# All three earlier taps of a causal convolution on TensorE; shorter rings, and one product per chunk from POOL to VectorE

## The chip, the cores and the metric

One core of one Trainium2 chip runs the whole kernel in one launch, in float32. The metric is device time in microseconds, median of the runs. Engines are named as in the profile: PE is TensorE, PEld its weight loads, DVE VectorE, ACT ScalarE, POOL GpSimd, SP SyncE.

## The reference, cut to what matters

```python
h = layernorm(x) * (1 + ca) + sa                     # x: (2, 2048, 512)
h, gate = split(h @ in_proj_w.T)                     # E = 1024 channels each
h_c = conv(h, conv_w, taps=4, causal, per channel) + conv_b
h = silu(h_c)
dt, B, C = split(h @ x_proj_w.T)                     # 128, N = 16, 16
dt = softplus(dt @ dt_proj_w.T + dt_proj_b)
s[t] = s[t-1] * exp(dt[t] * A) + dt[t] * h[t] * B[t] # E x N states
y = sum_n(s[t] * C[t]) + h * D
x = x + ga * ((y * silu(gate)) @ out_proj_w.T)
x = x + gb * (layernorm(x) * (1 + cb) + sb) @ sum_r(factors[r]) / sqrt(8)   # + bias
```

The convolution has four taps per channel: `h_c[t] = w3 h[t] + w2 h[t-1] + w1 h[t-2] + w0 h[t-3] + b`.

## The kernel before, in words

The 2 x 2048 rows are cut into 16 chunks of 256 rows, in order of time, eight for each batch. A chunk is worked in 64 units: a unit is one of the 16 state indices n of one of four pairs of channel blocks (2 x 128 channels). Two units are a step s (32 steps a chunk), four are a quad g (16 quads a chunk). While the units of chunk c run, the same program carries the input side of chunk c+1 (projection, convolution, silu, dt, B and C) and the output side of chunk c-1 (gate, output projection, residual, second norm, the last matrix product). What stands at which step is written out by hand in tables and conditions on s and g; each engine runs its own list strictly in that order and waits on semaphores.

A unit goes like this. POOL makes `ub` = u * B for a whole quad at once (`make_ub`, two quads ahead, ring of three). ScalarE makes the decays exp(dt * A) in one of three PSUM banks (`decays`). VectorE runs the scan over 256 rows (`scan`, line 1426). The state is multiplied by C either on VectorE (`multiply_c`, line 1441, into `sc_d`, ring of three) or, for the last k units of a quad, on POOL (line 596, into `state_p`, ring of `P_RING` slots). The tables `EVEN_POOL`, `ODD_POOL` and so on give k for each quad; chunk 0 has FIRST_POOL, chunk 1 FOLD_POOL, chunk 15 LAST_POOL, and chunks 2 to 14 take EVEN and ODD in turn (2 is even). TensorE turns every product with a transposing matmul and adds it up in `y_bank` (`turn_states`, line 1010), and ScalarE copies the sum of a pair to `y_rows` (line 811).

The convolution of pair q of chunk c+1 passes four engines. TensorE projects h into PSUM (`project_h`, line 1085). ScalarE copies it to `pre` with the last three rows of the chunk before, and scales the PSUM bank by w3 and adds the bias (`copy_h`, line 775; it sets `pre_made`). VectorE adds the tap w0 (`taps`, line 1481, two instructions of 256 columns; `tap_done`). TensorE adds w1 and w2: for each of two channel blocks a matmul of 256 columns for each tap, with a diagonal matrix of the weights as the stationary side (`add_tap`, line 1068). ScalarE takes the tanh (line 787), VectorE finishes the silu into `hc` (`silu_before`, line 1490). For pairs 0 to 3 in the chunks after the first, `copy_h` and `taps` stand at steps 5, 7, 11, 13, `add_tap` at 6, 8, 12, 14, tanh and silu at 8, 10, 14, 16. The next `project_h` into a bank waits for that silu.

On the output side of chunk c-1, TensorE turns the summed y (`turn_sums`, line 1141, steps 4 to 7), VectorE gates it (`gate_sums`, line 1522), TensorE projects it out (`project_out`, line 1157, steps 9 to 15), and VectorE adds the residual (`residual_mixer`, line 1529, steps 15 and 17).

POOL also makes u = dt * h for each pair (`make_u`, line 545), three of them in groups 0, 2 and 3 of a chunk and one in group 13 for the next.

Of the kernel before, what the change touches and what calls it, by code (L numbers as in the profile page):

```python
# [22 lines left out]
ALU = mybir.AluOpType  # L23
# [4 lines left out]
E, N, TAPS, RANK_DT = 1024, 16, 4, 128  # L28
RANK = 8
EPS = 1e-5  # L30
ROWS = 256
# [4 lines left out]
PAIRS = KE // 2  # L36
# [3 lines left out]
QUAD = 4  # L40
QUADS = UNITS // QUAD
UB_RING = 3
D_RING = 3
DVE_TAPS = 1
PE_TAPS = range(DVE_TAPS, TAPS - 1)
TAP_STEPS = 2 * DVE_TAPS
H_RING = 3
# [5 lines left out]
SILU_AT = ({7: 0, 9: 1, 12: 2, 14: 3}, {8: 0, 10: 1, 14: 2, 16: 3})  # L53
P_RING = 8
U_PAIRS = 3
H_TILES, Z_TILES = 3, 3
DT_PAIRS = 5
EVEN_POOL = (2, 2, 2, 2, 2, 2, 2, 2, 2, 2, 2, 1, 1, 1, 1, 1)
ODD_POOL = (2, 2, 2, 2, 1, 2, 2, 2, 2, 2, 2, 1, 1, 1, 1, 1)
FIRST_POOL = (2, 2, 1, 1, 1, 1, 1, 2, 1, 1, 1, 1, 1, 1, 1, 1)  # L60
# [104 lines left out]
def build(nc, x, win_m, xp_t, dt_t, wo_t, chan, cond_t, wmod, factors, bias, out):  # L165
# [11 lines left out]
    with ExitStack() as ctx:  # L177
# [6 lines left out]
        def sem(name):  # L184
            return ctx.enter_context(nc.semaphore(name))
# [82 lines left out]
        xa_loaded, bn_a, stats_a, norm_a, z_a = sem("xa_loaded"), sem("bn_a"), sem("stats_a"), sem("norm_a"), sem("z_a")  # L268
        pre_made, tap_done, tapped, diag_made, tanh_h_made, skip_made = sem("pre_made"), sem("tap_done"), sem("tapped"), sem("diag_made"), sem("tanh_h_made"), sem("skip_made")
        pair_read = sem("pair_read")  # L270
# [29 lines left out]
        def h_lane(c, q):  # L300

            return bank_c[q % 2] if c == 0 and q >= 2 else bank_a[q % 2]
# [210 lines left out]
        def _(pool):  # L513
# [27 lines left out]
            def make_u(c, q):  # L541

                pair, k = PAIRS * c + q, slice(2 * q, 2 * q + 2)
                pool.wait_ge(dt_made, pair + 1)
                pool.tensor_tensor(u[:, pair % U_PAIRS, :, :], dt[:, pair % DT_PAIRS, :, :], hc[:, k, :], ALU.mult).then_inc(u_made, 1)

# [103 lines left out]
            def one_round(c, par, la, lc):  # L650
                for g in range(QUADS):
# [9 lines left out]
                    multiply_c(quad)  # L661
                    if g in (0, 2, 3):
                        make_u(c, max(g, 1))
                    if c == 0 and g in (4, 6, 8, 10, 12, 14):
# [328 lines left out]
        def _(pe):  # L993
# [67 lines left out]
            def add_tap(c, q):  # L1061

                if c == 0 and q == 0:
                    pe.wait_ge(diag_made, len(PE_TAPS))
                pe.wait_ge(tap_done, TAP_STEPS * (PAIRS * c + q + 1))
                for j in range(2):
# [341 lines left out]
        def _(dve):  # L1408
# [61 lines left out]

            def taps(c, q):

                bk = h_lane(c, q)
                dve.wait_ge(pre_made, PAIRS * c + q + 1)
                for k in range(DVE_TAPS):
                    for j in range(2):
                        e, part = 2 * q + j, bk[:, j * ROWS:(j + 1) * ROWS]
                        if k:

                            dve.wait_ge(tap_done, TAP_STEPS * (PAIRS * c + q) + 2 * (k - 1) + j + 1)  # L1480
                        dve.scalar_tensor_tensor(out=part, in0=pre[q % 2][:, j, k:k + ROWS], scalar=conv[:, e, k:k + 1],  # L1481
                                                 in1=part, op0=ALU.mult, op1=ALU.add).then_inc(tap_done, 1)

            def silu_before(c, q):
# [118 lines left out]
            last.then_inc(seam_zeroed, 1)  # L1603
            taps(0, 0)
            for q in range(1, PAIRS):
                taps(0, q)
                silu_before(0, q - 1)
# [7 lines left out]
            def one_round(c, par, la, lc):  # L1615
                for s in range(STEPS):
# [52 lines left out]
                    if la is not None:  # L1669
                        if a in SILU_AT[c > 0]:  # L1670
                            silu_before(c + 1, SILU_AT[c > 0][a])
                        if a in TAP_AT[c > 0]:
                            taps(c + 1, TAP_AT[c > 0][a])
                    if la is not None and s == 31:
# [55 lines left out]
```

## Time and profile before

| | |
|---|---|
| median of 3 runs | 2022.62 us (2021.11 to 2022.76) |
| the profiled execution, its time | 2025.55 us |
| its span, first to last instruction | 2023.8 us |
| mean granted TensorE clock | 0.973 |
| instructions | 29343 |

The span is what the trace covers; the time of an execution has about 1.8 us around it. A row of a timeline gives start, duration, engine, line and tiles; brackets give how long the engine stood idle before it and what released it. One matmul of the program stands as two records in the trace, so that a row with x8 is four matmuls. PEclk is the granted clock: 1.00 is 2.4 GHz and 0.50 is 1.2 GHz, and a window that mixes them has a value between. Busy time of a full engine can be less than its work, since starts overlap the end of the instruction before.

### The profile page before, as it was taken

To read this page: it belongs to the slowest core of one execution; us is meant where nothing else is said; L and a number is where in the kernel's file an instruction comes from. 1 tells how busy PE (TensorE), PEld (TensorE's weight loads), DVE (VectorE), ACT (ScalarE), POOL (GpSimd) and SP (SyncE) were. 2 spreads that over 40 slices of the span, in tenths; PEclk is the share of its full clock that TensorE was granted. 3 is DMA by queue.
4 is the path that set the end of the run, shared out by engine and by line. 5 is a ranking of instruction groups with operands and counts; after the bars stand their busy time and mean duration, and the time that the engine had idled before them with its cause. 6 is when DMAs were issued, how large, how long until landed. Compare 5 with 4: busy or idle time off the path is not lost.

```text
span 2023.8 us, 29343 instructions
## 1 busy us (share of the span) xinstructions
PE 1759.7 (87%) x9128; PEld 1312.2 (65%) x9128; DVE 1867.4 (92%) x2240; ACT 1517.1 (75%) x4646; POOL 1835.7 (91%) x925
## 2 busy tenths in 40 slices
PE   7985889889889898988989888898988899898798
PEld 5664757667576765757666675766757576676564
DVE  2799989999999999999999999999999999999995
ACT  3767778697877869777786977878787786878662
POOL 1789999999999999999998999999999999999992
PEclk9897999999999999999999999999999999999798
DMA  4656514132140412304042240403223040311200
GB/s 171 235 114 153 140 48 147 31 121 79 43 143 15 152 47 97 103 30 154 17 141 68 111 141 22 157 22 131 68 73 121 28 156 22 121 53 55 92 27 32
DMA packets 72001, 186.17 MB, mean 92 GB/s; under 512 B 6818, under 2 KB 8482, under 8 KB 63908
## 3 DMA queue, kind: packets, MB, share of 16 engines
q1 hardware_dynamic: 68148, 176.95, 26.3%
q0 software_dynamic: 3696, 7.34, 2.2%
q8 instruction: 73, 1.20, 0.2%
q14 instruction: 84, 0.69, 0.1%
HBM read 172.20 MB, written 12.06 MB: 91 GB/s over the span
## 4 chain that ended last, share of the span: by engine, by line
PE 42%; ACT 19%; POOL 15%; DVE 13%; issue 9%; DMA 1%; DVEq 0%; POOLq 0%; SPq 0%; ACTq 0%
PE y_bank L1010 10%; PE bank_a L1085 10%; PE bank_c L1157 9%; POOL ub L568 8%; ACT decay L722 7%; DVE decay L1426 5%; POOL state_p L596 5%; PE bank_c L1057 4%; DVE state_p L1426 3%; PE bank_a L1068 2%; ACT dt L835 2%; DVE sc_d L1441 2%; ACT L722 2%; ACT hT L737 2%; ACT L835 2%
## 5 line engine op out<-in xcount | busy, mean ns | idle before, releaser
L568 POOL TENSOR_TENSOR ub<-u,b_all 128x2048 f32<-128x2048 f32 x255 | 1160.4, 4551 | 48.5 <-DMA b_all<-bc_scratch 47.4
L722 ACT ACTIVATE decay<-dt,decay_rate 128x256 f32<-128x256 f32 (+1 forms) x2048 | 889.6, 466 | 36.0 <-DVE state_p L1426 34.3
L1426 DVE TENSOR_TENSOR_SCAN decay<-decay,carry,ub 128x512 f32<-128x512 f32 x610 | 763.7, 1277 | 25.8 <-ACT decay L722 23.8
L596 POOL TENSOR_TENSOR state_p<-state_p,c_all 128x1024 f32<-128x1024 f32 (+1 forms) x256 | 498.7, 1948 | 85.3 <-ACT carry L706 82.4
L1426 DVE TENSOR_TENSOR_SCAN state_p<-decay,carry,ub 128x512 f32<-128x512 f32 x414 | 527.4, 1274 | 9.3 <-ACT decay L722 7.2
L1010 PE MATMUL y_bank<-ident,sc_d 128*128 128x128 f32 x2440 | 362.5, 283 | 79.9 <-DVE sc_d L1441 79.5
L1441 DVE TENSOR_TENSOR sc_d<-decay,c_all 128x512 f32<-128x512 f32 x610 | 406.7, 671 | 0.0
L1010 PEld LDWEIGHTS y_bank<-ident,sc_d 128*128 128x128 f32 x2440 | 292.9, 145 | 146.1 <-DVE sc_d L1441 120.8
L706 ACT ACTIVATE carry<-decay 128x2 f32<-128x2 f32 x610 | 100.8, 165 | 264.8 <-DVE sc_d L1441 262.9
L1010 PEld LDWEIGHTS y_bank<-ident,state_p 128*128 128x128 f32 x1656 | 195.7, 143 | 126.9 <-POOL state_p L596 71.7
L1010 PE MATMUL y_bank<-ident,state_p 128*128 128x128 f32 x1656 | 231.0, 279 | 53.2 <-POOL state_p L596 52.0
L1085 PE MATMUL bank_a<-hT,win_h 128*128 128x256 f32 x992 | 240.5, 387 | 32.4 <-DVE hc L1490 30.0
L1057 PE MATMUL bank_c<-hT,win_z 128*128 128x256 f32 x960 | 230.7, 387 | 0.0
L1157 PE MATMUL bank_c<-wo,yg 128*128 128x512 f32 x480 | 223.8, 594 | 0.0
L1085 PEld LDWEIGHTS bank_a<-hT,win_h 128*128 128x128 f32 x992 | 182.3, 193 | 58.7 <-DVE hc L1490 35.7
L1057 PEld LDWEIGHTS bank_c<-hT,win_z 128*128 128x128 f32 x960 | 181.7, 196 | 22.6
L1068 PE MATMUL bank_a<-pre_z,tap_diag 128*128 128x256 f32 x496 | 120.4, 386 | 12.2 <-DVE bank_a L1481 12.2
L1157 PEld LDWEIGHTS bank_c<-wo,yg 128*128 128x128 f32 x480 | 86.6, 191 | 67.0 <-issue 64.8
L1068 PEld LDWEIGHTS bank_a<-pre_z,tap_diag 128*128 128x128 f32 x496 | 92.7, 191 | 39.8 <-DVE bank_a L1481 15.8
L1187 PE MATMUL bank_c<-ffn,hT 128*128 128x512 f32 x240 | 115.9, 605 | 0.0
L1001 PE MATMUL y_bank<-ident,skipped 128*128 128x128 f32 x256 | 42.9, 294 | 71.5 <-ACT y_rows L811 71.5
L718 ACT ACTIVATE decay<-ident 128x1 f32<-128x1 f32 x608 | 103.4, 170 | 0.1
(139 smaller groups left out, 1842.1 us busy)
## 6 DMA issues: line engine op xcount, KB each, us to landing
win_h<-win_m SPq DMA_DIRECT2D x128, 256.0 KB, 2.6
win_z<-win_m SPq DMA_DIRECT2D x128, 256.0 KB, 2.8
b_all<-bc_scratch SPq DMA_DIRECT2D x31, 1024.0 KB, 4.7
c_all<-bc_scratch SPq DMA_DIRECT2D x31, 1024.0 KB, 6.6
xa<-x SPq DMA_DIRECT2D x16, 512.0 KB, 5.0
xc<-x SPq DMA_DIRECT2D x16, 512.0 KB, 3.8
out<-xc SPq DMA_DIRECT2D x15, 512.0 KB, 4.0
ffn<-factors POOLq DMA_DIRECT2D x7, 1024.0 KB, 10.0
```

The source lines that it names most:

```text
L568: pool.tensor_tensor(ub[:, slot, :, :, :], u[:, (PAIRS * c + q) % U_PAIRS, :, :].unsqueeze(1).to_broadcast([P, QUAD, 2, ROWS]), b_all[:, n ...
L596: pool.tensor_tensor(part, part, c_all[:, n + QUAD - k:n + QUAD, :].unsqueeze(2).to_broadcast([P, k, 2, ROWS]), ALU.mult).then_inc(pooled, 1)
L718: act.activation(bk[:, ROWS:ROWS + 1], ident[:, 0:1], ACT.Copy, scale=0.0)
L722: last = act.activation(bk[:, j * ROWS + j:(j + 1) * ROWS], dt[:, pair % DT_PAIRS, j, j:], ACT.Exp, scale=decay_rate[:, e, n:n + 1])
L1010: last = pe.matmul(y_bank[:, at:at + P], tile[:, j, t * P:(t + 1) * P], ident[:, :], start=False, stop=last_of_pair, is_transpose=True, sk ...
L1057: last = pe.matmul(dst[:, j * ROWS:(j + 1) * ROWS], tile[:, k, :], hTc[:, k, :], start=(k == 0), stop=(k == KD - 1))
L1068: last = pe.matmul(h_lane(c, q)[:, j * ROWS:(j + 1) * ROWS], tap_diag[:, i, 2 * q + j, :], pre[q % 2][:, j, k:k + ROWS], start=False, stop ...
L1085: last = pe.matmul(h_lane(c, q)[:, j * ROWS:(j + 1) * ROWS], win_h[i % H_TILES][:, k, :], hT[c % H_RING][:, k, :], start=(k == 0 and j == ...
L1157: last = pe.matmul(bank_c[t][:, :], yg[:, k, t * P:(t + 1) * P], wo[:, k, :], start=(k == 0), stop=(k == KE - 1))
L1187: last = pe.matmul(bank_c[t][:, :], hT[c % H_RING][:, k, t * P:(t + 1) * P], ffn[:, k, :], start=False, stop=(k == KD - 1))
L1426: dve.tensor_tensor_scan(dst, bk[:, :], ub[:, quad % UB_RING, i, :, :].rearrange("p j r -> p (j r)"), carried_in[:, n, 2 * q:2 * q + 1], A ...
L1441: dve.tensor_tensor(sc_d[:, i % D_RING, :, :], bk[:, :].rearrange("p (j r) -> p j r", j=2), c_all[:, n:n + 1, :].to_broadcast([P, 2, ROWS] ...
```

## The change

The last VectorE tap goes to TensorE: `PE_TAPS` is now all of 0, 1, 2, and `add_tap` waits for `pre_made` instead of `tap_done`. `taps` and its semaphore are gone. `tap_diag`, the store of the diagonals, grows by one tap (4 KB a partition), and two rings shrink by 2 KB each: `P_RING` from 8 slots to 7, u from three pairs to two. With two pairs, `make_u` has a wait of its own on the sums made from the pair it overwrites, and the u of pair 3 is made in group 6 instead of 3. The tables for chunks 2 to 14 change: an even chunk has one product at quad 3 (was two), an odd one has one at quads 3 and 7 and two at quad 4 (was two, two and one); each such chunk has one product less on POOL and one more on VectorE.

```diff
-DVE_TAPS = 1
-PE_TAPS = range(DVE_TAPS, TAPS - 1)
-TAP_STEPS = 2 * DVE_TAPS
+PE_TAPS = range(TAPS - 1)
...
-P_RING = 8
-U_PAIRS = 3
+P_RING = 7
+U_PAIRS = 2
...
-EVEN_POOL = (2, 2, 2, 2, 2, 2, 2, 2, 2, 2, 2, 1, 1, 1, 1, 1)
+EVEN_POOL = (2, 2, 2, 1, 2, 2, 2, 2, 2, 2, 2, 1, 1, 1, 1, 1)
...
                 pool.wait_ge(dt_made, pair + 1)
+                if pair >= U_PAIRS:
+
+                    pool.wait_ge(ub_made, N // QUAD * (pair - U_PAIRS + 1) - 1)
...
-                    if g in (0, 2, 3):
-                        make_u(c, max(g, 1))
+                    if g in (0, 2, 6):
+                        make_u(c, {0: 1, 2: 2, 6: 3}[g])
...
-                pe.wait_ge(tap_done, TAP_STEPS * (PAIRS * c + q + 1))
+                pe.wait_ge(pre_made, PAIRS * c + q + 1)
...
-            def taps(c, q):
-
-                bk = h_lane(c, q)
-                dve.wait_ge(pre_made, PAIRS * c + q + 1)
-                for k in range(DVE_TAPS):
-                    for j in range(2):
-                        e, part = 2 * q + j, bk[:, j * ROWS:(j + 1) * ROWS]
...
-                        if a in TAP_AT[c > 0]:
-                            taps(c + 1, TAP_AT[c > 0][a])
```

On TensorE, from the first tap group of an even chunk (step 6) to the end of step 9, before the change; `y_rows` is the turned sum of chunk c-1, `sc_d` and `state_p` the products from VectorE and POOL:

```order
L1068 MATMUL bank_a<-pre_z,tap_diag 128x256 x4
L1010 MATMUL y_bank<-ident,sc_d 128x128 x4
L1141 MATMUL bank_c<-ident,y_rows 128x128 x4
L1010 MATMUL y_bank<-ident,state_p 128x128 x8
L1010 MATMUL y_bank<-ident,sc_d 128x128 x4
L1141 MATMUL bank_c<-ident,y_rows 128x128 x4
L1068 MATMUL bank_a<-pre_z,tap_diag 128x256 x4
L1085 MATMUL bank_a<-hT,win_h 128x256 x4
L1010 MATMUL y_bank<-ident,state_p 128x128 x8
L1001 MATMUL y_bank<-ident,skipped 128x128 x4
L1010 MATMUL y_bank<-ident,sc_d 128x128 x8
```

and of the change:

```order
L1069 MATMUL bank_a<-pre_z,tap_diag 128x256 x6
L1011 MATMUL y_bank<-ident,sc_d 128x128 x4
L1142 MATMUL bank_c<-ident,y_rows 128x128 x4
L1011 MATMUL y_bank<-ident,state_p 128x128 x8
L1011 MATMUL y_bank<-ident,sc_d 128x128 x8
L1142 MATMUL bank_c<-ident,y_rows 128x128 x4
L1069 MATMUL bank_a<-pre_z,tap_diag 128x256 x6
L1086 MATMUL bank_a<-hT,win_h 128x256 x4
L1011 MATMUL y_bank<-ident,state_p 128x128 x4
L1002 MATMUL y_bank<-ident,skipped 128x128 x4
L1011 MATMUL y_bank<-ident,sc_d 128x128 x8
```

Each tap group has six matmuls for four, and the four transposes of unit 14's product stand at step 7, among those of VectorE's products, instead of at step 9 among POOL's.

On VectorE, at step 7 and 8 of the same chunk, before the change; `yg<-bank_c` is the gating, `hc` the silu:

```order
L1426 SCALAR_TENSOR_TENSOR state_p<-decay,carry,ub 128x512
L1441 TENSOR_TENSOR sc_d<-decay,c_all 128x512
L1426 SCALAR_TENSOR_TENSOR state_p<-decay,carry,ub 128x512
L1522 TENSOR_TENSOR yg<-bank_c,yg 128x512
L1481 SCALAR_TENSOR_TENSOR bank_a<-pre_z,conv,bank_a 128x256 x2
L1426 SCALAR_TENSOR_TENSOR decay<-decay,carry,ub 128x512 x2
L1441 TENSOR_TENSOR sc_d<-decay,c_all 128x512
L1522 TENSOR_TENSOR yg<-bank_c,yg 128x512
L1490 SCALAR_TENSOR_TENSOR hc<-tanh_s,bank_a 128x512
```

and of the change:

```order
L1427 SCALAR_TENSOR_TENSOR decay<-decay,carry,ub 128x512
L1442 TENSOR_TENSOR sc_d<-decay,c_all 128x512
L1427 SCALAR_TENSOR_TENSOR state_p<-decay,carry,ub 128x512
L1442 TENSOR_TENSOR sc_d<-decay,c_all 128x512
L1510 TENSOR_TENSOR yg<-bank_c,yg 128x512
L1427 SCALAR_TENSOR_TENSOR decay<-decay,carry,ub 128x512 x2
L1442 TENSOR_TENSOR sc_d<-decay,c_all 128x512
L1510 TENSOR_TENSOR yg<-bank_c,yg 128x512
L1478 SCALAR_TENSOR_TENSOR hc<-tanh_s,bank_a 128x512
```

The two tap instructions are gone, and a second product stands ahead of the gating, since unit 14 is now scanned in a decay bank and multiplied by VectorE.

## Rows read from the trace of the kernel before

**Rows 1.** The page: span and busy time of each engine.

```profile
span 2023.8 us, 29343 instructions
...
PE 1759.7 (87%) x9128; PEld 1312.2 (65%) x9128; DVE 1867.4 (92%) x2240; ACT 1517.1 (75%) x4646; POOL 1835.7 (91%) x925
```

**Rows 2.** Groups by line and shape: count, busy us, mean ns, idle before.

```profile
L1441 DVE TENSOR_TENSOR sc_d<-decay,c_all 128x512 f32<-128x512 f32 x610 | 406.7, 671 | 0.0
L596 POOL TENSOR_TENSOR state_p<-state_p,c_all 128x1024 f32<-128x1024 f32 x158 | 372.8, 2359 | 66.4 <-ACT carry L706 63.5 <-DVE decay L1426 2.7
...
L596 POOL TENSOR_TENSOR state_p<-state_p,c_all 128x512 f32<-128x512 f32 x98 | 126.0, 1285 | 18.9 <-ACT carry L706 18.9
...
L545 POOL TENSOR_TENSOR u<-dt,hc 128x512 f32<-128x512 f32 x63 | 80.3, 1275 | 0.0
...
L1481 DVE SCALAR_TENSOR_TENSOR bank_a<-pre_z,conv,bank_a 128x256 f32<-128x256 f32 x124 | 54.0, 481 | 21.3 <-ACT bank_a L775 21.3
```

**Rows 3.** VectorE timelines, 747 to 992: start us, us, instructions.

```profile
751.37 0.69 DVE L1529 TENSOR_TENSOR xc<-bank_c,xc 128x512 f32<-128x512 f32 x1 [0.95 <-PE bank_c L1157]
...
827.75 0.69 DVE L1522 TENSOR_TENSOR yg<-bank_c,yg 128x512 f32<-128x512 f32 x1 [0.39 <-PE bank_c L1141]
...
831.90 0.87 DVE L1481 SCALAR_TENSOR_TENSOR bank_a<-pre_z,conv,bank_a 128x256 f32<-128x256 f32 x2
...
854.35 0.88 DVE L1481 SCALAR_TENSOR_TENSOR bank_a<-pre_z,conv,bank_a 128x256 f32<-128x256 f32 x2 [0.75 <-ACT bank_a L775]
...
869.78 0.69 DVE L1529 TENSOR_TENSOR xc<-bank_c,xc 128x512 f32<-128x512 f32 x1 [0.95 <-PE bank_c L1157]
...
989.88 0.69 DVE L1529 TENSOR_TENSOR xc<-bank_c,xc 128x512 f32<-128x512 f32 x1 [0.95 <-PE bank_c L1157]
```

**Rows 4.** TensorE timelines, 832 to 925 and 1041 to 1070.

```profile
836.97 1.99 PE L1085 MATMUL bank_a<-hT,win_h 128*128 128x256 f32 x8 [2.15 <-DVE hc L1490]
838.80 1.04 PE L1010 MATMUL y_bank<-ident,state_p 128*128 128x128 f32 x8
840.62 0.63 PE L1001 MATMUL y_bank<-ident,skipped 128*128 128x128 f32 x4 [0.78 <-ACT y_rows L811]
...
854.04 1.89 PE L1068 MATMUL bank_a<-pre_z,tap_diag 128*128 128x256 f32 x8
...
869.58 1.03 PE L1102 MATMUL bank_a<-hc,xp 128*128 128x256 f32 x4
...
1048.23 0.98 PE L1001 MATMUL y_bank<-ident,skipped 128*128 128x128 f32 x4 [2.04 <-ACT y_rows L811]
```

**Rows 5.** Chain that ended last, 800 to 925: start us, us, what.

```profile
831.99 0.79 DVE bank_a L1481 x2
...
870.61 0.89 PE y_bank L1010 x8
```

**Rows 6.** Windows near the starts of chunks 5, 6, 7 and 15.

```profile
core 0: us, PE busy (x) PEld busy (x) DVE busy (x) ACT busy (x) POOL busy (x), PEclk, DMA share, GB/s
...
689.00:695.00 6.00, 5.33 (x25) 4.90 (x26) 5.92 (x7) 3.85 (x14) 5.03 (x5) 0.72 0.64 226
809.00:815.00 6.00, 5.25 (x33) 4.82 (x34) 5.92 (x7) 4.96 (x19) 5.05 (x5) 1.00 0.80 271
927.00:933.00 6.00, 4.83 (x21) 4.26 (x22) 5.92 (x8) 3.96 (x14) 5.03 (x5) 0.72 0.74 255
...
1884.00:1890.00 6.00, 5.85 (x28) 5.30 (x29) 6.00 (x8) 3.86 (x15) 4.94 (x4) 0.72 0.59 208
```

**Rows 7.** Chain that ended last in the opening.

```profile
32.55 1.73 PE bank_a L1068 x8
...
45.70 2.00 PE bank_c L1068 x8
```

**Rows 8.** POOL timeline, 800 to 925.

```profile
873.36 2.36 POOL L596 TENSOR_TENSOR state_p<-state_p,c_all 128x1024 f32<-128x1024 f32 x1 [1.81 <-ACT carry L706]
```

**Rows 9.** A window over the ends of chunks 0 and 1, columns as in rows 6.

```profile
135.00:305.00 170.00, 128.64 (x669) 97.03 (x668) 157.07 (x176) 119.92 (x376) 168.38 (x82) 0.92 0.42 109
```

More of the change, by code:

```diff
@@ L53 @@
 SILU_AT = ({7: 0, 9: 1, 12: 2, 14: 3}, {8: 0, 10: 1, 14: 2, 16: 3})
-P_RING = 8
-U_PAIRS = 3
+P_RING = 7
+U_PAIRS = 2
 H_TILES, Z_TILES = 3, 3
 DT_PAIRS = 5
-EVEN_POOL = (2, 2, 2, 2, 2, 2, 2, 2, 2, 2, 2, 1, 1, 1, 1, 1)
-ODD_POOL = (2, 2, 2, 2, 1, 2, 2, 2, 2, 2, 2, 1, 1, 1, 1, 1)
+EVEN_POOL = (2, 2, 2, 1, 2, 2, 2, 2, 2, 2, 2, 1, 1, 1, 1, 1)
+ODD_POOL = (2, 2, 2, 1, 2, 2, 2, 1, 2, 2, 2, 1, 1, 1, 1, 1)
 FIRST_POOL = (2, 2, 1, 1, 1, 1, 1, 2, 1, 1, 1, 1, 1, 1, 1, 1)
@@ L268, in build @@
         xa_loaded, bn_a, stats_a, norm_a, z_a = sem("xa_loaded"), sem("bn_a"), sem("stats_a"), sem("norm_a"), sem("z_a")
-        pre_made, tap_done, tapped, diag_made, tanh_h_made, skip_made = sem("pre_made"), sem("tap_done"), sem("tapped"), sem("diag_made"), sem("tanh_h_made"), sem("skip_made")
+        pre_made, tapped, diag_made, tanh_h_made, skip_made = sem("pre_made"), sem("tapped"), sem("diag_made"), sem("tanh_h_made"), sem("skip_made")
         pair_read = sem("pair_read")
@@ L1469, in stats_before @@
                 stats(c, xa, stat_a, bn_a, stats_a)
-            def taps(c, q):
-                bk = h_lane(c, q)
-                dve.wait_ge(pre_made, PAIRS * c + q + 1)
-                for k in range(DVE_TAPS):
-                    for j in range(2):
-                        e, part = 2 * q + j, bk[:, j * ROWS:(j + 1) * ROWS]
[L1478 to L1482, printed above, removed]
             def silu_before(c, q):
@@ L1603, in _ @@
             last.then_inc(seam_zeroed, 1)
-            taps(0, 0)
             for q in range(1, PAIRS):
-                taps(0, q)
                 silu_before(0, q - 1)
```

## The prediction

> **What bounds the kernel now.** I began with the page. By busy time VectorE is fullest (92%), POOL next (91%), TensorE 87% [rows 1], and it would follow that work taken off VectorE is time gained. That is an average, so I looked at one plain chunk, chunk 6, in VectorE's timeline. A chunk's pace can be read from the wait before the residual addition of line 1529, which comes once in each: 751.37, 869.78, 989.88, so 118.41 us for one chunk and 120.10 us for the next [rows 3]. The wait before each is 0.95 us, and its releaser is TensorE (bank_c, line 1157), not POOL or ScalarE. So at step 17 of each chunk VectorE is early and TensorE late. TensorE's timeline says how long it has been so: it waited 2.15 us for VectorE's silu at 836.97, then 0.78 us for the copy of y at 840.62, and from there nothing stands in brackets until the projection is over at 869.58 [rows 4]; 29 us of work back to back. The chain of waits agrees: it passes from VectorE's tap (0.79 us at 831.99), through the silu to TensorE, and is still on TensorE at 870.61 [rows 5]. The chunk is therefore a relay: VectorE from the gating at 827.75 (itself 0.39 us late by TensorE, [rows 3]) to the silu at step 8; TensorE from there to step 17; then VectorE, ScalarE and POOL mixed to the next chunk's start. What the change does is worth what it does inside these sections.
>
> **Taps off VectorE.** A pair of tap instructions takes 0.79 us in the chain [rows 5], 0.87 as timed alone [rows 3], so starts follow 0.08 us before ends. Four pairs a chunk are 3.16 us; over 16 chunks' worth of taps 51 us of starts. Where they lie decides. The pair of step 5 lies ahead of the gating that already waits for TensorE: gain nothing, the 0.39 us wait becomes 1.18. The pair of step 7 (831.90) lies in VectorE's own section: gain 0.79. The pairs of steps 11 and 13, with the 0.75 us wait for ScalarE before the second [rows 3], lie in TensorE's section: gain nothing, the 0.95 us wait grows.
>
> **One product from POOL to VectorE.** A product on VectorE lasts 0.67 us [rows 2], 0.59 with the same overlap; on POOL two together last 2.359 and one 1.285 us, so one less is 1.07 us [rows 2]. In even chunks it is unit 14, at step 7: VectorE's section becomes 0.59 longer, so with the tap 0.20 us shorter. TensorE's turning of it moves from step 9 to step 7, ahead of the section it bounds: eight records take 0.89 us [rows 5], four 0.44, so its section opens 0.44 us shorter. In odd chunks unit 14 moves the same way, unit 18 moves back to POOL (within the section, nothing) and unit 30 moves to VectorE at step 15: 0.44 us more in TensorE's section.
>
> **Third tap on TensorE.** The eight records of a tap group (four matmuls) take 1.73 us in the chain [rows 7]; six matmuls take 2.60, so 0.865 more each. The groups of steps 6 and 8 run into the pause that is now 2.15 us and mostly vanish in it. Those of steps 12 and 14 (the first at 854.04, [rows 4]) lie in the section back to back: 1.73 us more, with no cover. An even chunk is then -0.20 - 0.44 + 1.73 = 1.09 us longer, an odd one 1.53. Seven even and six odd plain chunks: 7.6 + 9.2 = **+16.8 us**. Bounds: below, 0.5 us a chunk (+6.5) if the later sections take back the rest in their small waits; above, the full 1.73 in each (+22.5).
>
> At this place a rule of the Trainium skill speaks for the change. Its page "Perfetto Trace Analysis", section "Identifying the Most-Contended Engine", says that matmul busy time is no measure of TensorE's headroom and that LDWEIGHTS busy share is one. By that TensorE has room for all the taps and only VectorE's share counts; it is the first rival below. The trace has weight loads at 65% and yet a VectorE that waits at step 17 for TensorE in chunk after chunk; I go by the waits.
>
> **The opening.** There is nothing there but the taps' chain: groups from 32.55 on, back to back with the projections, the last at 45.70 for 2.00 us [rows 7]. Four groups of 0.865 are 3.5 us more; VectorE's tap between copy and last group gives back the 0.36 us that TensorE had free before 45.70, and the rest of what it saves is covered. I take **+3.0**, bounds 1.5 and 3.5. The third diagonal on POOL is made long before its first use.
>
> **Chunks 0 and 1.** Here POOL is full: 168.38 of 170 us [rows 9]. VectorE's savings buy nothing while POOL's work stays (these chunks' tables are unchanged), and the product u of 1.275 us [rows 2] moves from group 3 to group 6, where POOL is busier. I take **+1**, bounds -6 (the taps' 3.16 us saved in both) and +4.
>
> **The rings.** With seven slots a slot is reused three quads later at the nearest, as before in some quads; TensorE turned that quad's products about two quads earlier, so no new wait: 0. The ring of two for u makes POOL wait only for sums that it made itself, at least a quad before: 0. In plain chunks POOL gets 1.07 us lighter and has waits to spend (1.81 us at 873.36, [rows 8]); a longer chunk gives it more. If this cover were gone, VectorE would wait for ub.
>
> **TensorE's clock.** Near a chunk's start TensorE pauses about 2.04 us for the copy of y; in chunk 8 the four transposes behind the pause took 0.98 us where the same took 0.63 at 840.62 [rows 4]. The granted clock there is 0.72 on average over 6 us in chunks 5, 7 and 15, and 1.00 in chunk 6 [rows 6]: the lower level, 1.2 GHz, for part of the stretch. Eight of the 14 chunks from 2 to 15 show 0.72, the first in chunk 5. A chunk with it is 120.10 - 118.41 = about 1.5 to 1.7 us longer. The change does not touch this pause, but it moves every chunk's start, and nothing in the profile says how often the fall then comes. I take three of 14, since the pause at step 8 shrinks and the pace alters: 5 x 1.5 = **-7.5 us**; bounds none (-12) and all 14 (+9).
>
> The page "TensorE: Matmul & The Clock Gate" of the Trainium skill, section "The HAM clock gate", has an idle array fall to 1.2 GHz and a busy one return to 2.4 GHz. The trace agrees with 0.72 behind a 2 us pause; by this rule alone fuller work helps.
>
> **Sum:** 16.8 + 3.0 + 1.0 - 7.5 = +13.3 us. The profiled execution took 2025.55 us (span 2023.8), so 2038.9; the median of the runs is 2.9 us under it, 2022.62, so **2036 us**.
>
> **Rivals.** (A) VectorE is the bound after all, and TensorE's lateness is only order, to be taken up elsewhere. For it: 92% busy. Each plain chunk loses 3.16 - 0.59 + 0.75 = 3.3 us: -43; chunks 0 and 1 -6, opening +3: 1977 us. It decides if TensorE has at least 1.73 us free between the silu and step 17; against it, it has none in brackets. 12%. This holds the skill's rule too.
> (B) The clock falls in as many chunks as now, or in more: 13.3 + 7.5 = +20.8, 2043 us, up to 2052. 18%.
> (C) The lengthening is half swallowed after step 17 and the clock hardly falls: 8 + 3 + 1 - 10 = about +2, 2025 us. For it: the small waits of that section; against: they belong to other chains. 18%.
> The forecast itself, 2031 to 2041, has 48%; 4% is left for what I don't see.
>
> **Numbers.** 0.2% is about what a measurement of this kernel can tell from no change, so 2018.6 to 2026.7 is "same". A lies wholly under it, and 2% of the rest; C gives 14% to "same" and the rest to slower. Range 2020 to 2048: A and the far end of B stay out.
>
> **What would show it.** Right: the wait of line 1529 for TensorE is about 4 us per chunk, VectorE's busy share falls below 91% while TensorE's passes 89%, silu's pause on TensorE shrinks to under 1.2 us, chunks without a clock fall last 119.5 us (even) and 119.9 (odd), the first scan comes 3 us later. Wrong: no wait at line 1529, or waits of VectorE for ub or for turned slots; or a count of clock falls far from three.

## The result and the profile after

The median went from 2022.69 us (2021.11 to 2024.16, 6 runs) to **2030.38 us** (2026.18 to 2031.85, 6 runs). The ratio is 1.0035, 95% interval 1.0022 to 1.0048: 7.7 us, or 0.35%, slower. The prediction was 2036 us with a range of 2020 to 2048. The direction was right and the size was not: 13.3 us forecast, 7.7 measured.

The page of the changed kernel, by its span and busy times, and from its groups (count, busy us, mean ns, idle before) the scan:

```profile
span 2028.5 us, 29843 instructions
...
PE 1796.2 (89%) x9384; PEld 1349.6 (67%) x9384; DVE 1829.1 (90%) x2125; ACT 1519.5 (75%) x4672; POOL 1822.7 (90%) x926
...
L1427 DVE TENSOR_TENSOR_SCAN decay<-decay,carry,ub 128x512 f32<-128x512 f32 x623 | 780.2, 1277 | 54.9 <-ACT decay L723 50.2
```

By busy time VectorE works 38 us less than before and POOL 13 us less [rows 1]; TensorE works 36.5 us more. Two engines got lighter, one got heavier, and the kernel got slower. The three heaviest engines now read 89, 90 and 90%: the busy shares alone say nothing about which of them sets the pace. VectorE's idle time ahead of the scans of this group is 54.9 us, and was 25.8 before.

**The chunk.** TensorE's timeline of the changed kernel over steps 7 to 9 of an even chunk, chunk 4, with the six matmuls of a tap group in each row of x12 (a transposing matmul stands in the trace as one record, unlike the others, so a row of 128x128 with x4 is the four transposes of one unit):

```profile
599.62 1.04 PE L1011 MATMUL y_bank<-ident,sc_d 128*128 128x128 f32 x8
600.49 0.60 PE L1142 MATMUL bank_c<-ident,y_rows 128*128 128x128 f32 x4
600.93 2.76 PE L1069 MATMUL bank_a<-pre_z,tap_diag 128*128 128x256 f32 x12
604.52 1.99 PE L1086 MATMUL bank_a<-hT,win_h 128*128 128x256 f32 x8 [0.83 <-DVE hc L1478]
606.35 0.60 PE L1011 MATMUL y_bank<-ident,state_p 128*128 128x128 f32 x4
607.73 0.63 PE L1002 MATMUL y_bank<-ident,skipped 128*128 128x128 f32 x4 [0.78 <-ACT y_rows L812]
...
621.15 2.76 PE L1069 MATMUL bank_a<-pre_z,tap_diag 128*128 128x256 f32 x12
```

It is to be compared with [rows 4]. The pause for VectorE's silu is 0.83 us instead of 2.15: the longer group ahead of it fills it. From there to the copy of y it is 607.73 - 604.52 = 3.21 us instead of 840.62 - 836.97 = 3.65, since unit 14's transposes have moved ahead: 0.44 shorter. The group of 621.15 is longer by 0.87 us with nothing that hides it.

VectorE's timelines of the changed kernel, at the end of step 6 (the gating ahead of unit 14's scan) and at steps 14 to 17 of chunk 4, and at step 17 of chunks 5, 6 and 7:

```profile
595.48 0.69 DVE L1510 TENSOR_TENSOR yg<-bank_c,yg 128x512 f32<-128x512 f32 x1 [1.01 <-PE bank_c L1142]
...
622.24 2.47 DVE L1427 TENSOR_TENSOR_SCAN decay<-decay,carry,ub 128x512 f32<-128x512 f32 x2 [2.13 <-ACT decay L723]
...
638.62 0.69 DVE L1517 TENSOR_TENSOR xc<-bank_c,xc 128x512 f32<-128x512 f32 x1 [2.36 <-PE bank_c L1158]
...
758.55 0.69 DVE L1517 TENSOR_TENSOR xc<-bank_c,xc 128x512 f32<-128x512 f32 x1 [1.99 <-PE bank_c L1158]
...
879.51 0.69 DVE L1517 TENSOR_TENSOR xc<-bank_c,xc 128x512 f32<-128x512 f32 x1 [2.36 <-PE bank_c L1158]
...
999.44 0.69 DVE L1517 TENSOR_TENSOR xc<-bank_c,xc 128x512 f32<-128x512 f32 x1 [1.99 <-PE bank_c L1158]
```

The residual addition (now line 1517) waits 2.36 or 1.99 us for TensorE where it waited 0.95 [rows 3]. Another 2.13 us has appeared earlier, behind a decay; it makes most of the growth of idle time ahead of the scans, 25.8 to 54.9 us. Its releaser is named ScalarE, but ScalarE itself was held by TensorE just before, as its own timelines show, of the kernel before (chunk 6) and of the changed one (chunk 4):

```profile
852.52 0.21 ACT L766 ACTIVATE pre_z<-hist 128x6 f32<-128x6 f32 x1 [0.78 <-PE bank_a L1085]
...
619.63 0.21 ACT L767 ACTIVATE pre_z<-hist 128x6 f32<-128x6 f32 x1 [1.38 <-PE bank_a L1086]
```

`copy_h` waits for the projection, and the decays stand behind it on ScalarE. The projection does not come later than before: from the chunk's first scan (802.75 before, 570.47 after) `copy_h` starts after 49.77 us before and 49.16 now. VectorE comes earlier still, having no taps at steps 11 and 13, and waits. Neither wait is new work: the time that VectorE saves comes out as waiting for TensorE. From the copy of y (607.73) to the residual (638.62) it is 30.89 us instead of 29.16 (840.62 to 869.78, [rows 3, 4]), so 1.73 more: two tap groups of 0.865, as worked out.

Chunk lengths here are from the first scan of one chunk to that of the next. By them chunks without a clock fall last 118.4 us before, and 119.5 (even) and 119.7 (odd) after, two of the even ones (8 and 14) 119.3.

**The clock.** Windows of 6 us near the starts of chunks 2, 4, 6 and 7 of the changed kernel, columns as in rows 6:

```profile
336.00:342.00 6.00, 5.42 (x26) 5.04 (x27) 5.93 (x7) 3.86 (x13) 5.06 (x5) 0.72 0.54 216
576.00:582.00 6.00, 4.53 (x29) 4.20 (x30) 5.92 (x8) 4.95 (x17) 5.04 (x4) 1.00 0.79 288
816.00:822.00 6.00, 5.33 (x25) 4.58 (x26) 5.92 (x7) 3.84 (x14) 5.03 (x5) 0.72 0.69 229
937.00:943.00 6.00, 5.14 (x32) 4.73 (x33) 5.93 (x7) 4.95 (x18) 5.04 (x5) 1.00 0.82 265
```

The granted clock falls to its lower level, 1.2 GHz, in chunks 2 and 6 and in no other of chunks 2 to 14; before it fell in 8 of these 13 (seven at this pause, once in chunk 3 behind the pause for the silu). Such a chunk lasts 1.6 to 1.7 us longer (121.2 us in chunk 6). Where the falls are is known of the profiled execution alone, but the mean granted clock of every run agrees: 0.978 to 0.982 in the six of the changed kernel, 0.972 to 0.976 in the 59 of the kernel before that were made beside the experiments.

In chunk 15 the clock stayed up at two places where it had fallen, and fell at three others as before. A window about 62 us from the chunk's start before:

```profile
1940.00:1946.00 6.00, 5.22 (x23) 4.67 (x22) 5.91 (x10) 3.79 (x13) 5.84 (x6) 0.50 0.01 3
```

and of the changed kernel at the start of chunk 15 and at the same place in it:

```profile
1893.00:1899.00 6.00, 5.30 (x32) 4.60 (x33) 6.00 (x8) 4.23 (x15) 4.87 (x5) 1.00 0.75 264
...
1949.00:1955.00 6.00, 5.22 (x34) 4.65 (x33) 5.91 (x10) 3.54 (x13) 5.84 (x5) 1.00 0.07 5
```

The start of chunk 15 was at 0.72 before [rows 6].

**The opening.** The chain that ended last, 31 to 51 us, of the changed kernel:

```profile
31.49 2.59 PE bank_a L1069 x12
...
47.04 2.59 PE bank_c L1069 x12
49.63 0.86 PE bank_a L1103 x4
```

The first group starts at 31.49 instead of 32.55 [rows 7], and the last ends at 49.63 instead of 47.70.

The whole span, by stage (us; falls of the clock taken with the chunks where they are):

| | before | after | difference | predicted |
|---|---|---|---|---|
| opening | 60.5 | 62.4 | +1.9 | +3.0 |
| chunks 0 and 1 | 265.3 | 267.1 | +1.8 | +1.0 |
| chunks 2 to 14 | 1552.2 | 1557.7 | +5.5 | +16.8 less the clock's share |
| chunk 15 | 145.8 | 141.2 | -4.6 | 0 (clock) |
| span | 2023.8 | 2028.5 | +4.7 | |

The two profiled executions differ by 4.7 us and the medians by 7.7, because the one of before was 2.9 us over its median and that of after (2030.22) at it.

### The profile page after: what moved, and what is told of

It reads as the page before. It is cut to its first block, busy times and chain, and to the rows that moved or that the text cites. A ratio compares the mean times of both kernels' runs of the same rounds, so it can differ in the third digit from the quotient of the medians.

```text
span 2028.5 us, 29843 instructions
## 1 busy us (share of the span) xinstructions
PE 1796.2 (89%) x9384; PEld 1349.6 (67%) x9384; DVE 1829.1 (90%) x2125; ACT 1519.5 (75%) x4672; POOL 1822.7 (90%) x926
## 4 chain that ended last, share of the span: by engine, by line
PE 44%; ACT 17%; DVE 16%; POOL 13%; issue 10%; DMA 0%; DVEq 0%; SPq 0%; ACTq 0%; POOLq 0%
PE bank_a L1086 10%; PE y_bank L1011 10%; PE bank_c L1158 9%; POOL ub L569 7%; DVE decay L1427 7%; ACT decay L723 6%; DVE state_p L1427 4%; PE bank_a L1069 4%; POOL state_p L597 4%; PE bank_c L1058 3%; DVE sc_d L1442 2%; ACT dt L836 2%; ACT hT L738 2%; ACT L723 2%; ACT L836 2%
## 5 line engine op out<-in xcount | busy, mean ns | idle before, releaser
L1427 DVE TENSOR_TENSOR_SCAN decay<-decay,carry,ub 128x512 f32<-128x512 f32 x623 | 780.2, 1277 | 54.9 <-ACT decay L723 50.2
L597 POOL TENSOR_TENSOR state_p<-state_p,c_all 128x1024 f32<-128x1024 f32 (+1 forms) x256 | 484.7, 1893 | 106.0 <-ACT carry L707 89.0
L1427 DVE TENSOR_TENSOR_SCAN state_p<-decay,carry,ub 128x512 f32<-128x512 f32 x401 | 510.7, 1274 | 7.5 <-ACT decay L723 5.5
L1442 DVE TENSOR_TENSOR sc_d<-decay,c_all 128x512 f32<-128x512 f32 x623 | 415.4, 671 | 2.5 <-PE y_bank L1011 2.5
L1011 PEld LDWEIGHTS y_bank<-ident,state_p 128*128 128x128 f32 x1604 | 189.2, 143 | 122.9 <-POOL state_p L597 66.8
L1011 PE MATMUL y_bank<-ident,state_p 128*128 128x128 f32 x1604 | 224.4, 278 | 49.0 <-POOL state_p L597 48.4
L1069 PE MATMUL bank_a<-pre_z,tap_diag 128*128 128x256 f32 x744 | 171.0, 379 | 1.1 <-ACT bank_a L776 1.1
L1069 PEld LDWEIGHTS bank_a<-pre_z,tap_diag 128*128 128x128 f32 x744 | 138.7, 190 | 31.4 <-issue 13.4
```

What stands on the lines that cost most here:

```text
L597: pool.tensor_tensor(part, part, c_all[:, n + QUAD - k:n + QUAD, :].unsqueeze(2).to_broadcast([P, k, 2, ROWS]), ALU.mult).then_inc(pooled, 1)
L1011: last = pe.matmul(y_bank[:, at:at + P], tile[:, j, t * P:(t + 1) * P], ident[:, :], start=False, stop=last_of_pair, is_transpose=True, sk ...
L1069: last = pe.matmul(h_lane(c, q)[:, j * ROWS:(j + 1) * ROWS], tap_diag[:, i, 2 * q + j, :], pre[q % 2][:, j, k:k + ROWS], start=False, stop ...
L1427: dve.tensor_tensor_scan(dst, bk[:, :], ub[:, quad % UB_RING, i, :, :].rearrange("p j r -> p (j r)"), carried_in[:, n, 2 * q:2 * q + 1], A ...
L1442: dve.tensor_tensor(sc_d[:, i % D_RING, :, :], bk[:, :].rearrange("p (j r) -> p j r", j=2), c_all[:, n:n + 1, :].to_broadcast([P, 2, ROWS] ...
```

## The experiments

What was open: whether TensorE's section between the silu and step 17 really is what lengthens the chunk, and not the new tables or the shorter rings; which taps are worth moving; and what part the clock has. In the theory of the prediction pairs 0 and 1 (steps 6 and 8) can go to TensorE at a gain, and pairs 2 and 3 (steps 12 and 14) only at a loss. The rivals were the tables, the rings, and the clock as what moves the time. Times are medians; a ratio is to the kernel before on the same chip, with its 95% interval.

**The change with the tables of before** (one product less on VectorE in each plain chunk).

```diff
-EVEN_POOL = (2, 2, 2, 1, 2, 2, 2, 2, 2, 2, 2, 1, 1, 1, 1, 1)
-ODD_POOL = (2, 2, 2, 1, 2, 2, 2, 1, 2, 2, 2, 1, 1, 1, 1, 1)
+EVEN_POOL = (2, 2, 2, 2, 2, 2, 2, 2, 2, 2, 2, 1, 1, 1, 1, 1)
+ODD_POOL = (2, 2, 2, 2, 1, 2, 2, 2, 2, 2, 2, 1, 1, 1, 1, 1)
```

> The change with the product tables of before (all taps on TensorE, rings of seven and two, no product moved). Theory 1 (a chunk is as long as VectorE's section to the silu of step 8 plus TensorE's section to the end of step 15): VectorE's section is 0.79 us shorter than in the kernel before, TensorE's 1.73 longer, so chunks without a clock fall last 119.3 us, both kinds, 0.2 and 0.4 less than in the change; about 2026 to 2027 us. Rival (the shorter rings or POOL are what costs): POOL has 1.07 us more per chunk, so the time is that of the change or over it, 2030 to 2040 us.

2026.21 us, 1.0022 (1.0013 to 1.0030). Chunks of 119.3 us for both kinds, two falls of the clock. The product costs 0.2 us in even and 0.4 in odd chunks, where 0.15 and 0.59 had been worked out. The rest of the loss is there without it: 119.3 is 0.9 above the 118.4 of before, where the taps alone give 1.73 - 0.79 = 0.94.

**The change with all first taps back on VectorE** (rings and tables of the change).

```diff
+DVE_PAIRS = (0, 1, 2, 3)
...
-                pe.wait_ge(pre_made, PAIRS * c + q + 1)
+                if q in DVE_PAIRS:
+                    pe.wait_ge(tap_done, 2 * (len(DVE_PAIRS) * c + DVE_PAIRS.index(q) + 1))
+                else:
+                    pe.wait_ge(pre_made, PAIRS * c + q + 1)
...
+                        if k == 0 and q in DVE_PAIRS:
+                            continue
...
```

(Left out: `taps` and its semaphore, back on VectorE for the pairs of `DVE_PAIRS`.)

> The change's rings and tables, but the first tap of all four pairs back on VectorE. Theory 1: against the kernel before only the product's move is left: VectorE's section 0.59 longer, TensorE's 0.44 shorter in even chunks, so 118.6 us (even) and 119.0 us (odd); 2024 to 2028 us with as many clock falls as before. Rival (rings and tables are the cost, the taps are not): 2030 us, as the change.

2021.69 us, 1.0005 (0.9996 to 1.0014), under the 2024 to 2028 expected. The six odd chunks from 3 to 13 had a fall (120.4 us), the even ones none (118.55, two of them 118.4). In the whole time the rings and the tables together cost nothing that the measurement can tell, but part of that is the clock: there are six falls for eight. The even chunks are 0.14 us longer than before, which is the product's 0.15 and leaves nothing for the rings. It is the taps that make the kernel slower.

**Only pairs 0 and 1 on TensorE** (`DVE_PAIRS = (2, 3)`) **and only pairs 2 and 3** (`DVE_PAIRS = (0, 1)`).

> The change, but only the groups of pairs 0 and 1 (steps 6 and 8) take the third tap on TensorE; pairs 2 and 3 have it on VectorE. Theory 1: the third tap on TensorE costs nothing in the pause, VectorE's tap nothing while it waits for TensorE: 117.8 us (even), 118.2 us (odd) without clock falls; 2015 to 2020 us, faster than both kernels. Rival (each tap on TensorE costs alike, wherever it stands): half way between the kernels, 2026 us.

> The mirror: only the groups of pairs 2 and 3 (steps 12 and 14) take the third tap on TensorE; pairs 0 and 1 have it on VectorE. Theory 1: the whole cost without the gain, 0.79 us more per chunk than the change: 120.3 (even) and 120.5 us (odd); 2038 to 2042 us, slower than both. Rival (each tap costs alike): 2026 us.

The second: 2054.41 us, 1.0161 (1.0148 to 1.0175). The chunks without a fall, all odd, last 120.5 us. Like is compared with like by the residual additions of step 17, of chunks 4 and 6, with one fall between them in either kernel; VectorE's timelines of the kernel with all four pairs on VectorE, then of this one:

```profile
630.15 0.69 DVE L1534 TENSOR_TENSOR xc<-bank_c,xc 128x512 f32<-128x512 f32 x1 [0.95 <-PE bank_c L1164]
...
869.13 0.69 DVE L1534 TENSOR_TENSOR xc<-bank_c,xc 128x512 f32<-128x512 f32 x1 [0.95 <-PE bank_c L1164]
...
642.10 0.69 DVE L1534 TENSOR_TENSOR xc<-bank_c,xc 128x512 f32<-128x512 f32 x1 [2.36 <-PE bank_c L1164]
...
884.54 0.69 DVE L1534 TENSOR_TENSOR xc<-bank_c,xc 128x512 f32<-128x512 f32 x1 [2.36 <-PE bank_c L1164]
```

238.98 us for two chunks against 242.44: 1.73 more in each, the prediction's figure. The time is longer than expected because the clock fell in nine of 13 chunks: 1582.9 us for chunks 2 to 14, where 13 x 120.5 is 1566.5. Five of the falls are at the pause near the chunk's start. The other four stand behind the silu's pause, which these pairs leave at 2.14 us; three of them make the chunk 123.2 to 123.4 us long.

The first: 2021.49 us, 0.9994 (0.9983 to 1.0005), no gain, where 2015 to 2020 had been expected. But in its profile the one chunk without a fall, chunk 2, lasted 117.8 us, as expected, less than in either kernel. All 12 others had a fall and lasted 119.3 to 119.7. Its runs lie far apart, 2015.1 us at a mean clock of 0.975 to 2025.1 at 0.970; the profiled one took 2023.8. TensorE's timeline of this kernel at the pause near the start of chunk 4:

```profile
569.42 0.60 PE L1012 MATMUL y_bank<-ident,state_p 128*128 128x128 f32 x4
572.06 0.63 PE L1003 MATMUL y_bank<-ident,skipped 128*128 128x128 f32 x4 [2.03 <-ACT y_rows L813]
572.52 1.37 PE L1012 MATMUL y_bank<-ident,sc_d 128*128 128x128 f32 x8
573.68 2.76 PE L1059 MATMUL bank_c<-hT,win_z 128*128 128x256 f32 x6
```

and a window over it, columns as in rows 6:

```profile
571.00:577.00 6.00, 4.94 (x22) 4.30 (x23) 5.92 (x8) 3.85 (x14) 5.04 (x5) 0.72 0.67 253
```

Behind the pause of 2.03 us, the first six records of a projection (the rest lies behind what is shown) take 2.76 us, where eight take 1.89 at full clock. The section model was right and its gain did not reach the time. If the clock took it, filling the pause must give it back. That was tried in two ways.

**The same with useless work in the pause** (the first half of a gate projection is computed twice, the first time without effect).

```diff
-            def turn_states(step):
+            def turn_states(step, between=None):
...
+                if between is not None:
+                    between()
...
-                    turn_states(STEPS * c + s)
+                    turn_states(STEPS * c + s, (lambda: project_gate(c - 1, 2, 0, again=True)) if lc is not None and s == 1 else None)
...
```

> Third tap on TensorE for pairs 0 and 1 only, and the four matmuls of one gate projection at step 0 done a second time in the pause of step 1, to no use: TensorE gets nothing done earlier, only the pause is smaller. Clock theory: chunks stay at 117.8 and 118.2 us but the falls go, which come in 12 of 13 chunks of the same kernel without it: 2003 to 2006 us against 2021. Rival (the chunk is held at 119.4 us by something else than the clock): 2021 us or a little over.

2004.60 us, 0.9913 (0.9900 to 0.9927). TensorE's timeline of this kernel at the same place in chunk 4, and its window:

```profile
566.95 1.89 PE L1061 MATMUL bank_c<-hT,win_z 128*128 128x256 f32 x8
569.14 0.63 PE L1003 MATMUL y_bank<-ident,skipped 128*128 128x128 f32 x4 [0.30 <-ACT y_rows L813]
```

```profile
568.00:574.00 6.00, 5.70 (x35) 4.86 (x35) 5.93 (x8) 4.95 (x17) 5.05 (x5) 1.00 0.68 267
```

The only difference to the kernel with the pause is more work for TensorE (and with it a tile of weights that is given back one step later), and this one is 16.9 us faster, or 16.4 by the ratios, since the two were run on different chips. No chunk from 2 to 14 has a fall; they last 117.8 (even) and 118.0 (odd). The even ones are as long as the one undisturbed chunk of the kernel with the pause, so the useless work changed nothing but the clock. How the same shows in the residual additions, their first start in chunk 1 and last in chunk 15, first with the pause:

```profile
L1534 DVE TENSOR_TENSOR xc<-bank_c,xc x30: 661/680/692, 262.3 to 1940.9; 128x512 f32<-128x512 f32 x30
```

and with the pause filled:

```profile
L1537 DVE TENSOR_TENSOR xc<-bank_c,xc x30: 664/683/692, 262.5 to 1919.6; 128x512 f32<-128x512 f32 x30
```

1678.6 against 1657.1 us.

**Useful work in the pause.** A gate projection that stood later in the same step is moved into the pause: of the changed kernel, of the one with pairs 0 and 1 alone, and of the kernel before.

```diff
-                    turn_states(STEPS * c + s)
+                    turn_states(STEPS * c + s, (lambda: project_gate(c - 1, 2, 1)) if lc is not None and s == 1 else None)
...
-                        if 0 <= s <= 3:
+                        if 0 <= s <= 3 and s != 1:
```

> The change, with the gate projection that stands behind the copy of y at step 1 put ahead of it, into TensorE's pause of 2.04 us. Theory 1 and the clock theory (the pause at the chunk's start is what lets the granted clock fall, and it lies on the way to VectorE's gating): no falls at units 4 and 5, VectorE's waits of 0.40 and 1.01 us at units 12 and 14 gone, chunks of 118.1 and 118.3 us; about 2009 us. Rival (the pause is harmless, chunks are bound elsewhere): 2030 us, as the change.

> Third tap on TensorE for pairs 0 and 1 only, and the pause of step 1 filled with the gate projection. Theory: chunks of 117.8 and 118.2 us without falls, less the waits of 0.40 and 1.04 us: 116.4 to 116.8; about 1985 us, well faster than before. Rival (falls are spread by chance and the section bound is elsewhere): 2015 to 2021 us.

> The kernel before with the same filling of the pause at step 1. Theory: chunks of 118.4 less the waits of 0.40 and 0.39 us = 117.6 us, no falls; about 1999 us, and the change with the filling (2009) stands 10 us over it. Rival: no gain, 2021 us.

The changed kernel: 2025.46 us, 1.0019 (1.0010 to 1.0028); no falls, chunks of 119.3 and 119.5. I had expected 2009, since VectorE's wait of 1.01 us at unit 14, and one of 0.40 at unit 12, should have gone. The second stayed and the first became 0.79; the timelines of this kernel in chunk 4, TensorE's at the pause and VectorE's at that gating:

```profile
575.81 0.63 PE L1002 MATMUL y_bank<-ident,skipped 128*128 128x128 f32 x4 [0.31 <-ACT y_rows L812]
...
578.60 0.66 PE L1011 MATMUL y_bank<-ident,sc_d 128*128 128x128 f32 x4 [1.29 <-DVE sc_d L1444]
...
593.59 0.69 DVE L1512 TENSOR_TENSOR yg<-bank_c,yg 128x512 f32<-128x512 f32 x1 [0.79 <-PE bank_c L1144]
```

The pause shrinks to 0.31 us, and 1.29 of the rest comes back a few matmuls later as a wait for a product from VectorE. The gating's wait and the chunk shrink by 0.2 us and no more: the rest of the pause was time in which TensorE was ahead of VectorE.

Pairs 0 and 1 alone: 2001.21 us, 0.9897 (0.9884 to 0.9911), no falls, chunks of 117.5 and 117.8 us. The expectation, 1985, carried the same error.

The kernel before: 2021.77 us, 0.9998 (0.9989 to 1.0007). The expectation, 1999, missed too. No falls at the filled pause in chunks 2 to 14, but ten at the next one, that for the silu at step 8, each 1.6 to 1.7 us. TensorE's timeline of this kernel there, in chunk 4, with the window:

```profile
592.02 1.99 PE L1070 MATMUL bank_a<-pre_z,tap_diag 128*128 128x256 f32 x8 [0.77 <-DVE bank_a L1483]
596.16 3.52 PE L1087 MATMUL bank_a<-hT,win_h 128*128 128x256 f32 x8 [2.15 <-DVE hc L1492]
```

```profile
592.00:598.00 6.00, 3.83 (x13) 2.97 (x14) 6.00 (x8) 1.91 (x7) 5.92 (x5) 0.87 0.00 2
```

The projection takes 3.52 us where it took 1.99 in [rows 4]. Filling one pause moved the fall to the other. In the changed kernel the second pause is 0.83 us, and in chunks 2 to 14 none of the eight profiled kernels with the longer tap group ahead of it (all with pairs 0 and 1 on TensorE) has a fall there.

**The kernel before with useless work in both pauses** (at step 1 the repeated gate projection as above, at step 8 this).

```diff
+                        if lc is not None and s == 8:
+                            project_out(c - 1, 0, 0, alone=True)
```

> The kernel before, with matmuls done a second time, to no use, in both of TensorE's pauses: one gate projection's at step 1 and the first output projection's at step 8. Nothing useful is done earlier. Clock theory: no falls, each of chunks 2 to 14 at 118.4 us, so 1539 us for the 13 against 1552: 2008 to 2010 us; the change's own cost without the clock is then 17 to 20 us, against the 8 us measured. Rival (the falls cost little): 2020 us.

2009.65 us, 0.9939 (0.9925 to 0.9953). Chunks 2 to 14 last 118.4 us (two of them 118.2), with no fall. So the falls cost the kernel before 12 to 13 us. This gives the change's own cost: compare this kernel with the changed one with its pause filled, also without falls: 1.0019 / 0.9939 = 1.0080, or 16 us. In the profiled executions it is more, 19.4, since that of this kernel was 3.0 us under its median; 12.9 of them are in chunks 2 to 14 (1551.5 against 1538.6). And pairs 0 and 1 alone, with their pause filled with useless work as well (0.9913), are faster than this kernel: 0.9913 / 0.9939 = 0.9974, 5 us, where without the filling they had shown no gain. With the intervals of both ratios it is 1 to 9 us; their five runs each do not overlap (2003.7 to 2005.0 against 2006.7 to 2011.1).

**The output projection into the pause of step 9, too** (pairs 0 and 1 on TensorE, both pauses for the copy of y filled with useful work), **and in a further kernel all output projections one step earlier.**

```diff
-                    turn_states(STEPS * c + s, (lambda: project_gate(c - 1, 2, 1)) if lc is not None and s == 1 else None)
+                    turn_states(STEPS * c + s, {1: lambda: project_gate(c - 1, 2, 1), 9: lambda: project_out(c - 1, 0, 0)}.get(s) if lc is not None else None)
...
-                        if 9 <= s <= 12:
+                        if 10 <= s <= 12:
```

> Third tap on TensorE for pairs 0 and 1 only, the gate projection ahead of the copy of y at step 1, and the first output projection ahead of the copy of y at step 9 (pause of 0.78 us inside TensorE's section). Theory 1: the section is 0.78 us shorter, chunks of 116.8 us, 10 us less than without the last edit: about 1991 us. Rival (VectorE or ScalarE bound there): 2001 us.

> As the kernel with both fillings, but the output projections stand one step earlier, the first at step 8 in the pause before VectorE's silu (0.83 us), the second ahead of the copy of y at step 9. Theory 1: up to 1.6 us off each chunk, until VectorE's 0.95 us of wait at line 1529 and its slack ahead are used up: 1980 to 1988 us. Rival: the first projection outlasts the pause by 0.9 us and delays the next input projection, 1991 us or over.

The first: **1989.25 us**, 0.9836 (0.9823 to 0.9850), the fastest kernel of this study. Chunks of 116.6 and 116.8, no falls. TensorE's timeline of this kernel, chunk 4, steps 8 and 9:

```profile
595.04 1.99 PE L1094 MATMUL bank_a<-hT,win_h 128*128 128x256 f32 x8 [0.83 <-DVE hc L1497]
596.87 0.60 PE L1012 MATMUL y_bank<-ident,state_p 128*128 128x128 f32 x4
597.31 1.88 PE L1166 MATMUL bank_c<-wo,yg 128*128 128x512 f32 x4
599.03 0.60 PE L1003 MATMUL y_bank<-ident,skipped 128*128 128x128 f32 x4
```

The 0.78 us wait for the copy is gone from TensorE's section, and the chunk is 1.0 shorter than with the pause at step 1 filled alone. Where the other 0.2 comes from was not looked for.

The second: 1993.49 us, 0.9859 (0.9845 to 0.9872), a miss: 4 us slower, where 1980 to 1988 had been expected and the rival said 1991 or over. Its residual addition, in VectorE's timeline, has no wait any more:

```profile
625.92 0.66 DVE L1536 TENSOR_TENSOR xc<-bank_c,xc 128x512 f32<-128x512 f32 x1
```

Chunks without a fall stayed at 116.6, and three had a fall near step 24, of 1.4 to 1.5 us each, which is the 4 us. With no wait for TensorE at step 17, earlier output from TensorE buys nothing.

## Why the prediction was right, and where its size was off

**The relay.** Right. The sections' lengths came as worked out: from the gating to the silu's end 0.18 shorter (0.20 forecast), to the copy of y 0.44 shorter (0.44), from there to the residual 1.73 longer (1.73). An even chunk is 1.1 us longer (1.09), an odd one 1.3 (1.53). That it is the taps was shown by putting them back (2021.69), and that it is those of steps 12 and 14 by moving the pairs apart: against all four on VectorE, pairs 0 and 1 take 0.8 us off an even chunk (117.8 for 118.55), pairs 2 and 3 add 1.73.

**Plain chunks, +16.8.** They gave 7 x 1.1 + 6 x 1.3 = +15.5 before the clock. The odd chunk's term was a little too large: the product at step 15 costs 0.4 and not 0.59.

**The clock, -7.5: the step that failed in size.** I took eight falls in chunks 2 to 15 and three of them left. There were nine behind these two pauses (I had missed that of chunk 3, behind the silu's pause), and one more that went, late in chunk 15; two were left, both at the pause for the copy of y. That gave about -10 in chunks 2 to 14 and, with both windows of chunk 15 back at 1.00, as it seems most of its -4.6, which no experiment took apart. This term is 7 us off. The plain chunks are 1.3 off the same way and the start of the kernel (below) 1.1, chunks 0 and 1 0.8 the other way: together the 8.6 us by which the span's +4.7 misses the sum of 13.3. The medians miss by less, 5.6, because the execution that the sum was made against lay 2.9 above its median and the prediction took the new one to do the same. How many falls to expect had no row in the profile; three was a guess, as its bounds said, and that two came is luck.

Between two kernels that both have no fall in chunks 2 to 14 the change costs 16 us, against 20.8 in the prediction's sum without its clock term; 2.6 of those 4.8 are the 0.2 us a chunk that filling the pause gave, and the rest is within the uncertainty of the two ratios.

**The opening, +3.0: 1.9.** The groups are longer by 0.86 us each as forecast: from the start of the first to the end of the last it is 18.14 us for 15.15, 2.99 more. The first starts 1.06 us earlier, and not by the change. TensorE's timelines, before and after, show the shift ahead of any tap, at the first projection:

```profile
23.72 8.83 PE L1085 MATMUL bank_a<-hT,win_h 128*128 128x256 f32 x32 [2.33 <-issue]
...
22.68 8.81 PE L1086 MATMUL bank_a<-hT,win_h 128*128 128x256 f32 x32 [2.32 <-issue]
```

The start varies between executions: the kernel before with one and with both pauses filled, whose opening is that of the kernel before, reached the first scan at 59.7 and 59.4 us, not 60.5. Against these two the opening of 62.4 is 2.8 and 3.0 longer. So the term was right, and the 1.1 us is the start of the profiled execution.

**Chunks 0 and 1, +1: 1.8.** Inside its bounds. Nearly all of it is in chunk 0 (139.9 us for 138.2). It wasn't taken apart.

**The rings, 0.** Right by the chunks' lengths: with the taps where they were, an even chunk is 0.14 us longer, the product's share. The whole time alone would not show it, since the clock fell less often there.

**What was to show it.** The wait at the residual addition came as 2.36 us and not about 4; the other 2.1 us stand at step 14, behind a decay. The sum is as forecast and the place was half wrong: `copy_h` waits for the projection and holds the decays up. VectorE fell to 90% as said; TensorE rose to 89% (88.5) and did not pass it. The silu's pause is 0.83, under 1.2. 119.5 was met; 119.9 was 119.7. The first scan came 1.9 us later and not 3, by the earlier start. The wait of unit 14's gating became 1.01, 1.18 forecast. In odd chunks VectorE also waits 0.41 us for a slot of `sc_d` that TensorE has yet to turn, just ahead of the residual's 1.99 (chunk 5); the prediction had named such a wait as a sign of being wrong, but here it is the same lateness of TensorE.

**The rivals.** A, VectorE as the bound, fell: 38 us less work on VectorE and a slower kernel. It needed 1.73 us free on TensorE between silu and step 17, and there is only the 0.78 us before the copy of y. The rule of the Trainium skill that the prediction set against the waits (page "Perfetto Trace Analysis", section "Identifying the Most-Contended Engine"), by which the weight loads' share tells TensorE's headroom, would have forecast it: the share is 67% here, and TensorE still set the pace. B (as many falls as before) fell too: 2 instead of 9 in chunks 2 to 15. C, 2025, is as near in time as the forecast, 2036 (5.4 and 5.6 us off), but by another way: nothing was swallowed behind step 17, the clock gave back more.

## What to carry to other kernels

When two engines hand a chunk back and forth, price a move by the section in which each instruction lies, not by the engine's total: the same edit, tap to TensorE, was worth -0.8 us a chunk at steps 6 and 8 and +1.7 at steps 12 and 14. Half of this change, the taps of steps 6 and 8 (with its rings and tables), is an improvement of about 5 us once the clock doesn't fall in either kernel. Look at TensorE's short pauses for their clock before believing a small difference: work moved into a pause, even useless work, gave 12 to 20 us in three kernels here, and an improvement can stay invisible until that is done. It gave 3 to 5 us where only two falls were left to lose, and nothing where the falls moved to the next pause.

## What was unexpected of the hardware

Behind a pause of about 2 us in TensorE's otherwise full stream the granted clock can fall: 0.72 on average over 6 us behind it, 1.6 to 1.7 us lost in the chunk. It does so after some of these pauses and not after others of the same length (2.04 us in the changed kernel's chunk 4, with 1.00 behind it). The page "TensorE: Matmul & The Clock Gate" of the Trainium skill, section "The HAM clock gate", has an idle array fall to 1.2 GHz and a busy one return; the repeated matmuls (2021.49 to 2004.60, and 2022.91 to 2009.65 us) agree with it.

Falls come and go with the pace of the loop. In four kernels whose chunks last between 117.8 and 118.6 us without a fall (the one before, all taps back, pairs 0 and 1 alone, the one before with one pause filled) chunks 2 to 14 take 1552.2, 1552.1, 1551.9 and 1552.4 us: 119.4 us a chunk on average in each, by 8, 6, 12 and 10 falls. The changed kernel, at 119.5 and above without one, has two. So a kernel made 0.6 us a chunk shorter had more falls and the same time. It is no rule, though: the kernel with pairs 2 and 3 alone has five falls at the same pause with chunks of 120.5 us, and the one with both pauses for the copy of y filled has none at 116.6. These are single executions, too: those of the kernel before and of pairs 0 and 1 alone were 2.9 and 2.4 us over their medians, the other two 1.4 and 0.8 under. Why the falls balance so closely in those four stays open.
